# Expert tiles listed by the first batch that fills them, rows gathered beside the expert loops

## The reference

```python
top_idx = argmax(x @ gate_w.T + gate_b + expert_bias)            # layer 1, 8 experts
out     = sum_e (top_idx == e) * (relu(x @ w1[e] + b1[e]) @ w2[e] + b2[e])
gate    = top-3 of softmax(x @ gate), renormalised                # layer 3, 16 experts
out     = sum_e gate[e] * (relu(x @ W1[e] + b1[e]) @ W2[e] + b2[e])
```

## Time and profile before

| | us |
|---|---|
| median of 3 runs (lowest, highest) | 650.31 (649.23, 650.84) |
| profiled execution, time | 652.92 |
| profiled execution, span | 651.1 |
| PE, DVE, ACT, POOL busy | 449.9, 341.3, 238.6, 212.5 |
| mean granted TensorE clock | 0.788 |

### The profile page before, as it was taken

How to read it: one execution, slowest core, us unless ns; L and a number is a source line. 1 busy time by engine, 2 the same in 40 slices (tenths; PEclk the granted TensorE clock), 3 DMA queues, 4 the chain that set the end, 5 groups by cost and what they waited for, 6 DMA issues and landing times.

```text
span 651.1 us, 9752 instructions
## 1 busy us (share of the span) xinstructions
PE 449.9 (69%) x2682; PEld 359.2 (55%) x2682; DVE 341.3 (52%) x1182; ACT 238.6 (37%) x628; POOL 212.5 (33%) x269
## 2 busy tenths in 40 slices
PE   3787866999058886400799899255379999996940
PEld 3664653999026775400687885023257677784730
DVE  4635364554146765320243444453567576867885
ACT  1111001666034642100476663123225654573511
POOL 5101173000460145775000004767352034463014
PEclk9985556999668995555799998776578999999655
DMA  7399972121840000111233331111000000000002
GB/s 200 58 375 346 403 307 65 49 66 34 264 137 2 0 21 30 48 53 49 83 102 106 99 106 50 49 49 38 16 20 2 0 2 2 1 1 1 1 1 65
DMA packets 58969, 53.68 MB, mean 82 GB/s; under 512 B 11458, under 2 KB 45203, under 8 KB 58788
## 3 DMA queue, kind: packets, MB, share of 16 engines
q1 hardware_dynamic: 52708, 43.62, 20.8%
q0 software_dynamic: 4096, 8.40, 4.1%
q10 hardware_dynamic: 2112, 1.05, 0.5%
HBM read 24.20 MB, written 28.84 MB: 81 GB/s over the span
## 4 chain that ended last, share of the span: by engine, by line
PE 39%; issue 27%; DVE 15%; ACT 5%; DVEq 4%; POOL 3%; DMA 3%; SPq 2%; another core or an unknown queue 1%; ACTq 0%; POOLq 0%
PE bank L1907 8%; PE bank L1894 7%; PE bank L1776 4%; PE bank L1792 2%; PE bank L1781 2%; ACT xn L1377 2%; SPq L345 2%; PE bank L1858 2%; POOL rstd L488 2%; DMA h_sb<-rowbuf 1%; PE bank L1886 1%; PE bank L1707 1%; PE bank L1624 1%; PE bank L1620 1%; DVE x L1064 1%
## 5 line engine op out<-in xcount | busy, mean ns | idle before, releaser
L1468 ACT ACTIVATE r<-bank,b 128x128 f32<-128x128 f32 x224 | 68.0, 367 | 28.8 <-PE bank L1894 28.7
L500 POOL DMA_INDIRECT rowbuf<-h_sb,slots x64 | 62.3, 973 | 29.9 <-issue 17.8
L1907 PE MATMUL bank<-wall,r 128*128 x448 | 68.5, 284 | 1.2 <-ACT r L1468 1.2
L487 POOL TENSOR_SCALAR nmr<-mv 128x4 f32<-128x4 f32 x32 | 7.9, 248 | 172.6 <-DVE veps L628 164.7
L511 POOL DMA_INDIRECT vZ<-rowbuf,slots x40 | 38.6, 964 | 73.0 <-DMA rowbuf<-h_sb 61.7
L1907 PEld LDWEIGHTS bank<-wall,r 128*128 128x128 f32 x448 | 57.3, 192 | 5.1 <-issue 2.1
L1894 PE MATMUL bank<-on,e_sb 128*128 128x128 f32 x352 | 53.6, 281 | 4.8 <-ACT on L1461 2.2
L1764 PE MATMUL bank<-ident,xn 128*128 128x128 f32 x64 | 13.5, 348 | 58.7 <-ACT xn L1377 58.5
L1075 DVE TENSOR_TENSOR h_sb<-bank,b2all 128x128 f32<-128x128 f32 x88 | 25.6, 291 | 52.2 <-PE bank L1907 52.0
L1792 PE MATMUL bank<-vB,eT 128*128 128x36 f32 x384 | 50.5, 281 | 2.1 <-ACT eT L1396 2.1
L1792 PEld LDWEIGHTS bank<-vB,eT 128*128 128x128 f32 x384 | 50.6, 206 | 2.2 <-ACT eT L1396 2.2
(11 more groups left out here) (259 smaller groups left out, 935.4 us busy)
## 6 DMA issues: line engine op xcount, KB each, us to landing
rowbuf<-zero SPq DMA_DIRECT2D x17, 1024.0 KB, 11.5
wall<-in_w SPq DMA_DIRECT2D x4, 2048.0 KB, 17.2
h_sb<-rowbuf SPq DMA_DIRECT2D x88, 64.0 KB, 1.8
rowbuf<-h_sb SPq DMA_DIRECT2D x88, 64.0 KB, 1.6
x<-in_x ACTq DMA_DIRECT2D x4, 256.0 KB, 5.5
rowbuf<-h_sb,slots POOLq DMA_INDIRECT x64
b2all<-in_L_ffn_b SPq DMA_DIRECT2D x1, 1024.0 KB
out<-h_sb SPq DMA_DIRECT2D x4, 256.0 KB, 2.6
```

The source lines that it names most:

```text
L500: nc.gpsimd.indirect_dma_start(rowbuf[0:MOE[l][0] * REGION * P], bass.IndirectOffsetOnAxis(slots[:, k * T + t:k * T + t + 1], 0), tile_of( ...
L1468: i = a.activation(hT[:, (u % 2) * 512 + c * P:(u % 2) * 512 + (c + 1) * P], bank[2 + u % 2][:, c * P:(c + 1) * P], ACT.Relu, bias=b1[l][: ...
L1907: y = mm(bank[6 + u % 2][:, 0:P], hT[:, (u % 2) * 512 + c * P:(u % 2) * 512 + (c + 1) * P], wall[:, bass.ds(e * n + (WHALF + c * P), P)], ...
```

## The change

- `slot_list` orders the tiles by the first batch that has a row in them, and by expert within that. For this `route` keeps the running counts after each batch (`seen`), and the list works on 4 x 8 or 4 x 16 segments. The count of tiles stays the same.
- `READY` is the number of tiles, at most, that hold rows of the batches up to b, rounded up to four: 12, 16, 20, 24 in layer 1 and 28, 40, 52, 64 in layer 3. `gather` waits for that many stored tiles only, so its indirect DMAs can run beside the loop.
- In layer 1 the sum and the statistics of batch 0 move into the loop, beside tile 21. In layer 3 the sum, statistics, norm and turn of batch 0 follow the loop.
- `prepare(4)` moves to before batch 3's turn and gating, using banks 2 and 6; `prepare(6)` moves to after `slot_list(3)`, ahead of loop 3.
- In attention 4 the sums of batches 1, 2, 3 move on DVE from tiles 1, 5, 8 to 1, 4, 8, and norm and turn to 1, 5, 9. POOL's order changes as shown.

```diff
+ADDED = {2: {3: 2, 6: 3}, 4: {1: 1, 4: 2, 8: 3}}
+TURNED = {2: {0: 1, 4: 2, 7: 3}, 4: {1: 1, 5: 2, 9: 3}}
+READY = {l: [-(-(((b + 1) * W * P * TOPK[l] + MOE[l][0] * (P - 1)) // P) // GT) * GT for b in range(B)] for l in MOE}
...
+            def gather(l, b, first, last):
...
-                        pool.wait_ge(s_ys[r], 16 * GT * (tile_before[l] + SLOT_TILES[l]) // BODY)
+                        groups = sum(1 for g in range(READY[l][b] // GT) if g % 2 == r)
+                        pool.wait_ge(s_ys[r], 16 * GT * (tile_before[l] // BODY + groups))
...
-            for b in range(2):
-                gather(1, b, 0)
-                gather(1, b, 1)
+            gather(1, 0, 0, 4)
+            gather(1, 1, 0, 4)
             power(8)
-            gather(1, 2, 0)
-            gather(1, 2, 1)
+            gather(1, 2, 0, 4)
             power(9)
...
-            gather(3, 0, 0)
-            gather(3, 0, 1)
-            gather(3, 1, 0)
+            gather(3, 0, 0, 12)
+            gather(3, 1, 0, 12)
+            pool.wait_ge(s_a, 4 * len(AL))
+            gather(3, 2, 0, 12)
             power(16)
-            gather(3, 1, 1)
-            pool.wait_ge(s_a, 4 * len(AL))
-            gather(3, 2, 0)
+            gather(3, 3, 0, 3)
             power(17)
-            gather(3, 2, 1)
-            gather(3, 3, 0)
+            gather(3, 3, 3, 12)
             power(18)
-            gather(3, 3, 1)
...
+                v.tensor_copy(seen[:, b * E:(b + 1) * E], base[:, 0:E])
...
+                for h in range(2):
+                    v.tensor_tensor(wide.rearrange("p (s m) -> p s m", m=8), rows.unsqueeze(2).to_broadcast([NS, G, 8]),
+                                    full[0:NS, 8 * h:8 * h + 8].unsqueeze(1).to_broadcast([NS, G, 8]), ALU.is_gt)
...
+                for b in range(B):
+                    summed = xn[0:NS, (b % 2) * 256:(b % 2) * 256 + E * E].rearrange("p (e f) -> p e f", e=E)
...
-                if l == 3:
-                    for later in (4, 6):
-                        for stage in range(6):
-                            prepare(later, stage)
-                    v.copy_predicated(cap6[:, :], mask_u8[:, :], neg3[:, :])
-                add_experts(l, 0)
-                stats_of(4 * l + 4, 0)
...
+                    if s == 21:
+                        add_experts(1, 0)
+                        stats_of(norm_no(2, 0), 0)
...
-            for b in (2, 3):
-                gating(3, b)
-                route(3, b)
+            gating(3, 2)
+            route(3, 2)
+            for stage in range(6):
+                prepare(4, stage)
+            gating(3, 3)
+            route(3, 3)
             slot_list(3)
+            for stage in range(6):
+                prepare(6, stage)
+            v.copy_predicated(cap6[:, :], mask_u8[:, :], neg3[:, :])
             moe(3)
+            add_experts(3, 0)
+            stats_of(norm_no(4, 0), 0)
```

More of the change, by code:

```diff
@@ L143, in build @@
         base0, base = sb("base0", 16), sb("base", 16)
[L144 to L148, removed]
+        seen = sb("seen", B * 16)
+        segs = {l: sb(f"segs{l}", 3 * B * MOE[l][0]) for l in MOE}
         at_f = sb("at_f", 2)
+        rest_f = sb("rest_f", 2)
+        place_f = sb("place_f", 2)
         of_f = sb("of_f", 2)
@@ L500, in scatter @@
                         nc.gpsimd.indirect_dma_start(rowbuf[0:MOE[l][0] * REGION * P], bass.IndirectOffsetOnAxis(slots[:, k * T + t:k * T + t + 1], 0), tile_of(xn_all, t), None).then_inc(s_sc_x, 16)
-            def gather(l, b, part):
+            def gather(l, b, first, last):
                 K = TOPK[l]
-                if b == 0 and part == 0:
+                if first == 0:
                     for r in range(2):
-                        pool.wait_ge(s_ys[r], 16 * GT * (tile_before[l] + SLOT_TILES[l]) // BODY)
[L508 to L511, removed]
+                        groups = sum(1 for g in range(READY[l][b] // GT) if g % 2 == r)
+                        pool.wait_ge(s_ys[r], 16 * GT * (tile_before[l] // BODY + groups))
+                for i in range(first, last):
+                    c = i % K * T + b * W + i // K
+                    nc.gpsimd.indirect_dma_start(tile_of(yg[l][b], i), None, rowbuf[0:MOE[l][0] * REGION * P], bass.IndirectOffsetOnAxis(slots[:, c:c + 1], 0)).then_inc(s_gat[b], 16)
             def add_bo(b):
@@ new lines, in part, with by_batch @@
+                def part(i, n=G):
+                    return ab[0:NS, i * 64:i * 64 + n]
+                def by_batch(i):
+                    return part(i).rearrange("p (b e) -> p b e", b=B)
+                rows, tiles, fresh, ends, hot = (part(i) for i in range(5))
+                reached, table = ab[0:NS, 320:320 + 2 * G], r5[0:NS, 0:2 * G]
+                total = part(7, B)
+                wide = xn[0:NS, 0:G * 8]
+                index, start, of = (segs[l][0:NS, i * G:(i + 1) * G] for i in range(3))
@@ new lines, in slot_list @@
+                v.tensor_tensor(rows.rearrange("p (b e) -> p b e", b=B), seen[0:NS, 0:G].rearrange("p (b e) -> p b e", b=B),
+                                base0[0:NS, 0:E].unsqueeze(1).to_broadcast([NS, B, E]), ALU.subtract)
+                v.tensor_copy(table[:, G:2 * G], of)
+                v.tensor_copy(table[:, 0:E], start[:, 0:E])
+                dve.drain()
+                for h in range(2):
+                    v.tensor_tensor(wide.rearrange("p (s m) -> p s m", m=8), rows.unsqueeze(2).to_broadcast([NS, G, 8]),
+                                    full[0:NS, 8 * h:8 * h + 8].unsqueeze(1).to_broadcast([NS, G, 8]), ALU.is_gt)
+                    dve.drain()
+                    v.tensor_reduce((tiles, hot)[h], wide.rearrange("p (s m) -> p s m", m=8), AX_X, ALU.add)
+                    dve.drain()
@@ L1406, in period @@
             def period(l, t):
[L1408 to L1411, removed]
+                if l in TURNED and t - 1 in TURNED[l]:
+                    turned(l, TURNED[l][t - 1])
                 if l == 6 and t == 4:
@@ L1443, in prepare @@
                     if l == 4:
-                        a.activation(kT[:, :], bank[0][:, 0:P], ACT.Identity, bias=bk[:, 0:1]).then_inc(s_kT, 1)
+                        a.activation(kT[:, :], key_bank(l, 0)[:, 0:P], ACT.Identity, bias=bk[:, 0:1]).then_inc(s_kT, 1)
                     else:
-                        a.copy(kT[:, :], bank[0][:, 0:P]).then_inc(s_kT, 1)
+                        a.copy(kT[:, :], key_bank(l, 0)[:, 0:P]).then_inc(s_kT, 1)
                 else:
@@ L1513, in _ @@
                 copy_logits(b)
+                for stage in range(5):
+                    prepare(2 * b, stage)
             moe(3)
@@ L1931, in moe @@
                 second(last, BODY - 1, False, experts[1])
[L1932 to L1935, removed]
                 turn_x(l + 1, 0)
@@ L1949, in _ @@
             project(2, 3)
[L1950 to L1953, removed]
+            turn_x(3, 2)
+            logits(3, 2)
+            ranks(3, 2)
+            for stage in range(5):
+                prepare(4, stage)
+            turn_x(3, 3)
+            logits(3, 3)
+            ranks(3, 3)
             slot_list(3)
+            for stage in range(5):
+                prepare(6, stage)
             moe(3)
@@ L2076, in constants, with segments @@
     e = np.arange(16)
+    def segments(E):
+        i = np.arange(B * E)
+        return np.tile(np.concatenate([i, i % E * REGION, i % E]).astype(f), (P, 1))
     return {
```

104 lines of the change are left out of this document (52 added, 52 removed).

## The result

The changed kernel took 662.5 us (661.2 to 667.8 in four executions; a fifth took 658.0), the kernel before 650.5 beside it: a ratio of 1.019, 95% interval 1.012 to 1.025. It was predicted at 622 and is slower. The same two kernels were later compared on other chips, where the changed one took 0.950 and 0.955 of the kernel before. "The record" is the first one. The profile of the changed kernel is that of its slowest execution (667.8 us, span 665.9).

What follows compares the result with a forecast made beforehand. POOL's gather queue was taken to delay the stage after each full expert loop, leaving holes. Terms summed to -27.9 us, giving 622 against the 650.3 median; the forecast's own range was 612 to 632, the wider range 606 to 642.

Steps and rivals of the forecast that it cites:

- gathers inside the loops: Gathers moved beside the loops cost 0.23 us each: +2.8 in loop 1 (12), +8.3 in loop 3 (36).
- gathers and loop serialise: Rival: each of 48 moved gathers stops the loop 1.26 us, 60.5 in place of 13.1, 670 us; chance 0.05.
- Tile loads: In loop 3, PE's waits for tile loads beside the gathers were put at +2 us.
- the rival that they give way: Tile loads in loop 3 give way to gathers: 31 us in place of 10.3, total 643; chance 0.17.
- POOL late through DVE's copies: Rival: each gather waits 0.29 us for a DVE weight copy, power(16) 5 us late, total 627; chance 0.08.
- Lists: Layer 1's list ordered by batch: +6.0 us; layer 3's list costs 12 us where it cost 3.4.
- the two holes: First scores come sooner after each loop's last bias: -18 us behind loop 1, -19 behind loop 3.
- Ahead of loop 3: Moved preparations and the longer list before loop 3 delay its start: +4.5 us (0 to 9).
- batch 1's chain: In attention 2, batch 1's norm no longer queues in POOL behind four gathers; DVE's wait before tile 4 mostly goes: -3 us.
- Attention 4, -12: Only batch 3's gathers run beside attention 4; fewer hitches, a shorter DVE wait and higher clock save 12 us (5 to 16).

Runs made afterwards that it cites:

- before_again: The kernel before, unaltered, run again on chip 13: 641.7 us, its loop 3 78.6 us.
- after_again: The changed kernel, unaltered, run again on chip 13: 607.5 us, ratio 0.950 to the kernel before; its loop 3 78.8 us.
- spaced kernels: The changed kernel with gathers paced by biases, 24 in loop 3 one per 1.5 tiles, batch 2's behind: ratio 0.963 (chip 9); layer 1's eight paced too: 0.965 (chip 12).
- after_d: The changed kernel, unaltered, on chip 9: 661.4 us in one execution beside 650.8 for the kernel before; loop 3 118.8 us.
- late3_c: The changed kernel with layer 3's gathers all behind loop 3, on chip 6: 634.4 us against 641.2 for the kernel before; loop 3 77.0 us.
- after_c: The changed kernel, unaltered, on chip 6: ratio 0.955 to the kernel before; loop 3 78.5 us.
- run 301: Not a label of a run: the text says that after_c "had run 301" of attention 2's matmuls, a count.

## Why the prediction was wrong

The parts of the span, before to after, against the terms. "Record" is the pair of profiles of the first result (652.9 and 667.8 us, so their difference is 15 and not the 12 of the medians), "chip 13" that of before_again and after_again (spans 636.6 and 604.9).

| part of the span | predicted | record | chip 13 |
|---|---|---|---|
| to loop 1's first bias (list) | +6.0 | +4.9 | +3.1 |
| loop 1 (batch 0's sum, gathers) | +3.3 | +3.6 | +0.5 |
| its last bias to the first scores | -18 | -19.2 | -19.0 |
| attention 2 and ahead of loop 3 | +1.5 | +7.3 | +2.7 |
| loop 3 (gathers, loads) | +10.3 | +42.3 | +0.2 |
| its last bias to the first scores | -19 | -20.0 | -19.4 |
| attention 4 to the end | -12 | -4.0 | +0.2 |
| sum | -27.9 | +14.8 | -31.7 |

**The step that failed** is "gathers inside the loops", "I take 0.23 each, the nearest row: ... +8.3 in loop 3". It measured 1.17 each in the record (42.3 / 36) and 1.11 on chip 9. The rival "gathers and loop serialise", with 1.26 each, gives nearly the size of what happened in loop 3, and it was given 0.05; but no gather stops the loop by itself, the first three of a burst do not. In loop 1 eight gathers in two bursts, and three at its very end, cost 3.6 us in the record, where 2.8 was put for twelve; on chips 9 and 12 the loop took 50.7 to 52.4 us with them so and 47.7 with the eight spread. The ground given against the rival, "they share only DMA engines", looked at the wrong resource: what came late was the word from PE to ACT and DVE, and this very hitch was in the trace of before. There it was averaged over 30 gathers, in a stage where PE ran at 0.73 to 0.75 clock with waits of its own. In a loop in which PE, ACT and DVE pass every tile on within a microsecond, the same hitch stops all three. A row from a stage with slack was used as a price in a stage without any.

**Tile loads** (+2, and the rival that they give way): not it. After the first tile PE waited for loads 2.7 us in the changed loop, where it had waited 2.6 before.

**POOL late through DVE's copies:** hardly seen. The gathers kept 1.25 us in the median beside the weight copies, on every chip, with single ones up to 1.47.

**Lists, the two holes:** the holes are right within 1.5 us, the lists within 3. The list itself takes 7.7 us where it took 2.7.

**Ahead of loop 3, and batch 1's chain:** +1.5 was predicted, +7.3 and +2.7 measured. In the record attention 2 grew from 64.0 us (first scores to last normalise) to 68.6, where -3 was expected; the -3 came nowhere. With it goes a lower clock, 0.82 against 0.89 in its first 58 us, and the last section shows such a difference on a chip without the disturbance; so this part may be none of the change's. Ahead of loop 3, DVE's sum of batch 3's slots waits 9.4 us without a releaser, beside scatters; the same wait is 4.2 us in the kernel before and 2.4 on chip 13.

**Attention 4, -12:** not met in either pair. On chip 13 it took 80 us before and after, with granted clocks of 0.67 and 0.84 before and 0.67 and 0.83 after in its halves. The clock was the same with fewer gathers beside it, and no hitches either way. In the record it fell from 86.7 to 81.5 us, near those 80: of the term only the hitches' part was there to be had, 5 of its 6.9 us. In the changed kernel of the record POOL's waits for DVE's variances and DVE's for the scores there are:

```profile
POOL nmr L494 <- DVE veps L629: 52.0, 5, 13.2
DVE bank L1035 <- PE bank L1809: 24.9, 4, 7.4
```

DVE has four waits for scores, one at each batch's first tile: 7.4, 6.0, 6.0 and 1.5 us before, 7.4, 6.0, 4.1 and 7.3 now. The wait of 6.01 us shrank by 1.9, and that for batch 3, whose norm and turn had moved from tile 8 to 9, grew by 5.8 (from 2.7 to 7.3 on chip 13). POOL now idles, 52 us in five waits, but PE still waits 5 to 7 us for each later batch's normalised rows.

**Where no disturbance is**, the predicted ratio, 622 / 650.3 = 0.956, stands beside 0.950 and 0.955, but by luck: two errors cancel. The loops pay 0.7 us and not 13.6, attention 4 gives nothing and not 12.

**Open:** what the chips differ in. Three (1, 6, 13) show the kernel before at 638 to 642 us and no such wait in any trace taken there; two (9, 12) and the record show 650 to 653, and waits without a releaser, most of 2 to 9 us, beside dense indirect DMAs, gathers and scatters alike. Which chip the record was taken on isn't known. No chip was seen twice, so the chip can't be told apart from whatever else differed at the time. Whether the index, the pieces of a gather or POOL's work on it is the cause wasn't tried on a disturbed chip: POOL arithmetic ran on chip 13 only, and a gather with fewer bytes per index wasn't run. That it is a backlog of gathers rests on the spaced kernels (0.26 against 1.11 us each) and on the first three gathers of a burst, beside which nothing is late; 24 dense ones weren't run beside this loop on chip 9.

## What to carry to other kernels

A hitch with no releaser in the trace is a price of something; find what it coincides with before more of that is moved beside a full loop, and price it there at its whole length, not at its mean over a slack stage. Indirect DMAs that fill a loop's idle queue are best spread by a wait on the loop's own count: that cost nothing that could be seen on chip 1 (78.4 us against 78.1 in a burst), and on chip 9 spreading, with the last twelve behind the loop, turned 118.8 us for 36 into 85.2 for 24. Before a result of some per cent is explained by the program, both kernels are best run again on another chip.

## What was not expected of the hardware

- The same two programs give 1.019 on one chip and 0.950 and 0.955 on two others. The kernel before alone differs by 2% (638.6 to 653.2).
- Beside dense gathers on some chips PE's results reach ACT and DVE up to 4.2 us late, while ACT's reached an idle PE within 0.15 us all through loop 3 of the record's changed kernel and of after_d.
- 36 plain loads at 0.54 us from POOL's queue did not do this on chip 12 (80.5 us).
- POOL additions double DVE's SBUF to SBUF copies (300 to 633 ns), yet the loop is only 3 us longer than in after_again (82.0 us against 78.8); DVE still waits 14.8 us for PE before them.
- The same stretch of code, from attention 2's first scores to loop 3, took 126.8 us in one execution on chip 6 and 134.9 in another, without a wait that has no releaser in either. PE's granted clock was 0.94 and 0.83 in attention 2's 58 us. Two rows, of late3_c and then of after_c:

```profile
171.40:230.00 58.60, 48.74 (x250) 36.44 (x250) 37.20 (x116) 27.72 (x56) 13.40 (x22) 0.83 0.31 98
```

```profile
169.90:228.00 58.10, 47.93 (x301) 37.20 (x301) 40.53 (x125) 30.39 (x62) 18.05 (x26) 0.94 0.32 105
```

In nearly equal time after_c had run 301 of attention 2's matmuls and late3_c 250.
